# Identity matmuls and a reordered Wo fold in the prologue, x2 transfers issued ahead of stores, and three down jobs among the last output projections of a decoder-layer kernel

## The reference

```python
q, k, v = heads(x @ Wq.T), heads(x @ Wk.T), heads(x @ Wv.T)      # 16 heads of 32
q_r, k_r, v_r = q @ Wdown, k @ Wdown, v @ Wdown                  # rank 32
attn = softmax(q_r @ k_r.T / sqrt(32))
out = heads_back((attn @ v_r) @ Wup) @ Wo.T
x = layernorm(x + out)
r[s] = decay * r[s-1] + ctx[s] * ctx[s]                          # per head, along the sequence
x = layernorm(x + x * r)
inter = silu(x @ gate_w.T) * (x @ up_w.T)                        # 512 -> 2048
x = layernorm(x + inter @ down_w.T)                              # 2048 -> 512
```

## Time and profile before

| | us |
|---|---|
| runs | 713.72, 713.31, 709.81 |
| median | 713.31 |
| profiled execution | 709.71 |
| its span, first to last instruction | 707.2 |
| PE busy | 657.8 (93%) |
| DVE busy | 442.3 |
| ACT busy | 348.5 |
| POOL busy | 289.2 |

### The profile page before, as it was taken

The page is one execution under the profiler, slowest core; times in us unless marked ns, Lnnn a source line. Parts: engine busy times, 40 slices in busy tenths (PEclk is TensorE's granted clock), DMA queues, the critical chain, the costliest instruction groups (busy, mean ns, idle before and its releaser), DMA issues.

```text
span 707.2 us, 11967 instructions
## 1 busy us (share of the span) xinstructions
PE 657.8 (93%) x4284; PEld 537.4 (76%) x4284; DVE 442.3 (63%) x827; ACT 348.5 (49%) x1001; POOL 289.2 (41%) x350
## 2 busy tenths in 40 slices
PE   6899999999999999999687789999999999999994
PEld 6678787887878887887555567888888888888883
DVE  2257667697676877868767676765554555454434
ACT  4555656556466675675655554653333334332220
POOL 0744475987639568485743642500010001000103
PEclk9999999999999999999989898999999999999998
DMA  9530101200212120121302362555163515440301
GB/s 330 182 125 31 61 1 31 90 32 1 90 61 91 40 69 12 61 70 41 99 1 68 96 156 70 115 146 126 31 172 88 127 30 164 99 97 0 120 0 59
DMA packets 22010, 58.04 MB, mean 82 GB/s; under 512 B 4033, under 2 KB 7233, under 8 KB 21057
## 3 DMA queue, kind: packets, MB, share of 16 engines
q1 hardware_dynamic: 16720, 44.45, 21.9%
q0 software_dynamic: 4944, 12.32, 5.9%
q10 hardware_dynamic: 288, 0.52, 0.3%
HBM read 32.11 MB, written 8.39 MB: 57 GB/s over the span
## 4 chain that ended last, share of the span: by engine, by line
PE 85%; DVE 6%; ACT 3%; DMA 2%; issue 1%; POOL 1%; SPq 1%; ACTq 0%; DVEq 0%; POOLq 0%
PE bank L302 21%; PE bank L303 19%; PE bank L304 19%; PE bank L486 7%; PE bank L508 5%; PE bank L474 5%; DVE minus_max L830 3%; PE bank L1201 2%; PE bank L1104 2%; DMA x_in<-x 1%; PE bank L494 1%; ACT probs L671 1%; PE bank L1173 1%; PE bank L399 1%; PE bank L525 1%
## 5 line engine op out<-in xcount | busy, mean ns | idle before, releaser
L671 ACT ACTIVATE probs<-bank,minus_max 128x256 f32<-128x256 f32 x256 | 117.2, 487 | 18.8 <-DVE minus_max L830 18.8
L302 PE MATMUL bank<-down,hidden_hi_lo 128*128 128x512 f32 x256 | 102.1, 399 | 0.0
L303 PE MATMUL bank<-down,hidden_hi_lo 128*128 128x512 f32 x256 | 101.0, 394 | 0.0
L304 PE MATMUL bank<-down,hidden_hi_lo 128*128 128x512 f32 x256 | 100.5, 392 | 0.0
L830 DVE TENSOR_REDUCE minus_max<-bank 128x2 f32<-128x512 f32 x128 | 79.4, 682 | 20.3 <-PE bank L474 20.3
L1402 DVE TENSOR_TENSOR hidden<-bank,silu 128x512 f32<-128x512 f32 x64 | 44.1, 690 | 63.5 <-PE bank L304 60.7
L1365 ACT ACTIVATE silu<-bank 128x512 f32<-128x512 f32 x64 | 38.3, 598 | 84.6 <-PE bank L304 83.7
L1406 DVE TENSOR_TENSOR hidden_hi_lo<-hidden,hidden_hi_lo 128x512 fp32r<-128x512 f32 x64 | 45.0, 703 | 41.2 <-ACT hidden_hi_lo L1378 41.1
L844 DVE COPY probsT<-bank 128x512 f32<-128x512 f32 x96 | 60.4, 682 | 10.9 <-PE bank L486 10.8
L1475 POOL TENSOR_TENSOR ffn_var_eps<-ffn_mean_var,constants 128x4 f32<-128x4 f32 x3 | 0.6, 198 | 158.9 <-DVE ffn_mean_var L1422 158.9
L486 PE MATMUL bank<-ident,probs 128*128 128x128 f32 x512 | 63.5, 278 | 2.0 <-ACT probs L671 2.0
(11 more groups left out here) (167 smaller groups left out, 1617.6 us busy)
## 6 DMA issues: line engine op xcount, KB each, us to landing
features_by_group<-features_by_cell SPq DMA_DIRECT2D x128, 128.0 KB, 2.4
ctx_squared_T<-in_ctxT SPq DMA_DIRECT2D x8, 512.0 KB, 3.3
xres<-in_x SPq DMA_DIRECT2D x8, 512.0 KB, 5.3
x_in<-x SPq DMA_DIRECT2D x16, 256.0 KB, 3.0
x_residual<-x POOLq DMA_DIRECT2D x4, 1024.0 KB, 9.1
out_x<-x_residual POOLq DMA_DIRECT2D x16, 256.0 KB, 2.8
xin_T<-in_xT SPq DMA_DIRECT2D x7, 512.0 KB, 4.2
x<-x_rows SPq DMA_DIRECT2D x7, 512.0 KB, 3.0
```

Of the source, the lines that this page charges most:

```text
L302: nc.tensor.matmul(out, wh, xh, start=first, stop=False)
L303: nc.tensor.matmul(out, wh, xl, start=False, stop=False)
L304: return nc.tensor.matmul(out, wl, xh, start=False, stop=last)
L671: inc(nc.scalar.activation(probs[:, g, t, :], S[g][:, t * T:(t + 1) * T], ACT.Exp, bias=nmax[:, g, t:t + 1], accum_out=rsum[:, t, g:g + 1] ...
```

## The change

Four parts.

1. **Prologue.** PE multiplies the identity by itself 14 times (`pe_warm`, into bank 4, read by nobody) as soon as the identity is there. The diagonals' two products move from PE's start to behind the first half of the K projection. Of the Wo fold one product stays ahead of the first transposes, two go behind them, one goes behind `pe_r`; ACT's copies of V and casts of Wo and DVE's low parts of Wo go behind the exponentials and the copies of the heads.
2. **x2 transfers.** In batch 7 SP issues `xres` and the x2 rows t = 2 and 3 first, and the store of batch 5 after them. For blocks 1 to 3 the rows t = 0 and 1 go between the two halves of the feature transfers of the block before. The transposes of rows t = 2 of block 0 move from head group 1 to head group 2 of batch 7.
3. **Hand-over to the FFN.** The function table with silu is loaded in batch 7, behind the exponentials of the last head group, by a one-column activation. The last product of the moments goes behind the running sum's transposes. Job 18 joins 16 and 17: one before, one between, one behind the two output projections.
4. **First step.** With three jobs made ahead, step 0 has two jobs instead of four, the second of them behind the gate and up products of j = 1. Each later step still has four until they run out, one job further on.

```diff
-    FOLD_O, XB = (A_, B_, C_, A_), (B_, A_, C_, C_)
+    FOLD_O, XB = (C_, B_, A_, C_), (B_, A_, C_, C_)
+    WARM = 14
+    def pe_warm(pe):
+        pe.wait_ge(s_ident, 1)
+        for i in range(WARM):
+            nc.tensor.matmul(bank[4][:, 0:P], ident[:], ident[:], start=True, stop=True)
...
 def pe_first_k(pe):
...
+            if k == 1:
+                pe_diagonals(pe)
...
 def pe_fold_o(pe, m):
         if m == 0:
             pe.wait_ge(s_wo, 16)
-            pe.wait_ge(s["vc"], 1)
-        elif m == 1:
+            pe.wait_ge(s["qwl"], 3)
+        elif m == 3:
+            pe.wait_ge(s["owl"], 1)
+        else:
             pe.wait_ge(s["vc"], 2)
-        elif m == 2:
-            pe.wait_ge(s["qwl"], 3)
-        else:
-            pe.wait_ge(s["owl"], 1)
...
 def act_batch(act, b):
...
         act_extra_hi(act, b, 2)
+        if not proj:
+            nc.scalar.activation(silu_ready[:], nmax[:, 0, 0:1], ACT.Silu)
         act_heads(act, b, 3)
...
 def sp_batch(sp, b):
...
+        if b == B - 1:
+            wait(sp, "r1", 2 * b)
+            inc(sp.dma_start(xres[:], x_v[:, b, :, :]), "xres", 16)
+            for t in range(2, BT):
+                sp_x2in(sp, 0, t)
+            sp_store(sp, b - 2)
+            return
...
-    AHEAD_JOBS = 2 * NG + 2
+    AHEAD_JOBS = 2 * NG + 3
...
 def pe_down(pe, step, t):
-                pe.wait_ge(s["wld"], 2 * JT * (g + 1) - 2)
+                pe.wait_ge(s["wld"], 2 * JT * g + 1)
...
 def job_of(n, g, k):
-        i = AHEAD_JOBS + 2 * JT * g + k
-        return i if n == 0 and i < NJOB else None
+        i = AHEAD_JOBS + (2 * JT * g - 2 + k if g else k)
+        return i if n == 0 and i < NJOB and (g or k < 2) else None
...
 def pe_step(pe, n, g):
         pe_down(pe, prev, 1)
-        pe_fill(pe, n, g, 1)
+        if prev:
+            pe_fill(pe, n, g, 1)
         pe_turn(pe, n, g, 1)
         pe_gate_up(pe, n, g, 1)
-        pe_fill(pe, n, g, 2)
+        pe_fill(pe, n, g, 2 if prev else 1)
...
             pe_rs(pe, B - 1, 0)
             pe_rs(pe, B - 1, 1)
-            pe_o(pe, B - 1, 0)
+            pe_features(pe, 0, 3, A_)
             pe.wait_ge(s["yv"], 4 * B)
             pe_job(pe, 2 * NG, X)
-            pe_o(pe, B - 1, 1)
+            pe_o(pe, B - 1, 0)
             pe.wait_ge(s["ws"], 2 * NG + 1)
             pe_job(pe, 2 * NG + 1, X)
+            pe_o(pe, B - 1, 1)
+            pe.wait_ge(s["ws"], 2 * NG + 2)
+            pe_job(pe, 2 * NG + 2, X)
```

More of the change, by code:

```diff
@@ L425, in pe_q @@
             pe.wait_ge(s["xl"], 2 * nb + 2)
-            pe.wait_ge(s["owl"], 3)
+            pe.wait_ge(s["owl"], 4)
             wait(pe, "rs1", 2 * nb - 3)
@@ L554, in pe_batch @@
         if b == 0:
-            for m in range(MT):
-                pe_fold_o(pe, m)
+            pe_fold_o(pe, 0)
         else:
@@ L561, in pe_batch @@
         pe_t(pe, b, 0)
+        if b == 0:
+            pe_fold_o(pe, 1)
+            pe_fold_o(pe, 2)
         if post:
@@ L567, in pe_batch @@
         pe_extra(pe, b, 0)
+        if b == 0:
+            pe_fold_o(pe, 3)
         pe_pv(pe, b, 0)
@@ L595, in pe_batch @@
         else:
+            pe_xt(pe, 0, 2, B_)
             pe_xt(pe, 0, 3, A_)
@@ L707, in act_batch @@
         if b == 0:
+            act_v(act, 0, 0)
+            act_v(act, 0, 1)
+        act_heads(act, b, 0)
+        if b == 0:
             for m in range(MT):
                 act_weight_hi(act, "o", m)
-        act_heads(act, b, 0)
         if post:
@@ L848, in dve_batch @@
         dve_max(dve, b, 0)
-        if b == 0:
-            for m in range(MT):
-                dve_weight_lo(dve, "o", m)
         dve_extra(dve, b - 1, 3)
@@ L859, in dve_batch @@
         dve_heads(dve, b, 0)
+        if b == 0:
+            for m in range(MT):
+                dve_weight_lo(dve, "o", m)
         dve_y(dve, b, 0)
@@ L873, in dve_batch @@
         dve_max(dve, b, 2)
-        if not proj:
-            dve_x2l(dve, 0, 2, B_)
         dve_extra(dve, b, 1)
@@ L1385, in act_step @@
         act_fill_hi(act, n, g, 0)
-        act_fill(act, n, g, 1)
-        act_turn(act, n, g, 1)
-        act_fill_hi(act, n, g, 1)
-        act_silu(act, n, g, 1)
+        if before(n, g):
+            act_fill(act, n, g, 1)
+            act_turn(act, n, g, 1)
+            act_fill_hi(act, n, g, 1)
+            act_silu(act, n, g, 1)
+        else:
+            act_silu(act, n, g, 1)
+            act_fill(act, n, g, 1)
+            act_fill_hi(act, n, g, 1)
         act_fill(act, n, g, 2)
@@ L1442, in dve_step @@
         dve_fill_lo(dve, n, g, 0)
-        dve_fill(dve, n, g, 1)
-        dve_turn(dve, n, g, 1)
-        dve_fill_lo(dve, n, g, 1)
-        dve_hm(dve, n, g, 1)
+        if before(n, g):
+            dve_fill(dve, n, g, 1)
+            dve_turn(dve, n, g, 1)
+            dve_fill_lo(dve, n, g, 1)
+            dve_hm(dve, n, g, 1)
+        else:
+            dve_hm(dve, n, g, 1)
+            dve_fill(dve, n, g, 1)
+            dve_fill_lo(dve, n, g, 1)
         dve_fill(dve, n, g, 2)
@@ L1653, in _ @@
                 sp_batch(sp, b)
-            for t in range(2, BT):
-                sp_x2in(sp, 0, t)
             for g in range(QUAD):
@@ L1659, in _ @@
             sp_store(sp, B - 2)
+            for t in range(2):
+                sp_x2in(sp, 1, t)
             for c in range(CELLS):
@@ L1663, in _ @@
             for n in range(1, NB):
-                for t in range(BT):
+                for t in range(2, BT):
                     sp_x2in(sp, n, t)
@@ L1670, in _ @@
                     sp_store(sp, B - 1)
+                if n + 1 < NB:
+                    for t in range(2):
+                        sp_x2in(sp, n + 1, t)
                 for c in range(CELLS):
```

15 lines of the change are left out of this document (7 added, 8 removed).

## The result

The changed kernel takes **689.37 us** (median of 4 runs, 689.23 to 690.51) against 712.56 us (709.81 to 713.72) for the kernel before, run on the same chip beside it: ratio 0.968, 95% interval 0.965 to 0.972. The forecast was 690.0 us. A second set on another occasion gave 689.34 against 710.61 us, 0.970 (0.968 to 0.972).

The account below looks back on a forecast made before the run. PE, busy for 93% of 707.2 us, was taken as the bound. Gains 5.1 + 5.2 + 4.5 + 6.7 = 21.5 us from the profiled 709.7 gave 688.2, plus 1.8 made 690.0; own spread 685.5 to 693, to 697 for 8 in 10.

Parts of the forecast that it names:

- Prologue: Start through batch 0's first attention times V, which would end at 37.0 instead of 42.1 us: gain 5.1 us.
- The order: Prologue: exponentials ahead of V copies and Wo casts, most Wo folds later; 4.0 of the prologue's 5.1 us.
- the warm-up: Kernel start: identity products let K's 48 matmuls pass at the fast pitch; net gain 1.1 us with the diagonals moved.
- The rival drawn from it: Kernel start: with only 6 slow matmuls the warm-up is worth 0.2 us and the sum 20.6; no chance given.
- x2 rows, block 0: Batch 7, head group 1: rows issued earlier end PE's 6.4 us wait; gain 5.2 us, clock included.
- block 1: FFN, x2 rows issued near 399 instead of 422.36 us: idle 4.7 and half of 4.0 go; gain 6.7 us.
- Hand-over and first step: Attention to FFN: first down product 8.7 us behind the first gate product; gain 4.5 us.
- The table load: Batch 7's last group: the 1.28 us silu load fits ACT's 1.45 us idle but for 0.1; with drain, sum 20.3.
- The 1.8 us between the profiled execution and the median: Whole kernel: half of the 3.6 us by which the median stood above the profiled execution, added to 688.2.
- The clock rival: Thinned stretches (31 to 36, 347 to 354, 389 to 398 us): two clock falls, about 2 us each, 692 to 695; chance 0.15.
- Holes only change their names: Prologue and hand-over lose as much as they win, only x2 parts pay (11.9): 697.8, median 699.6; chance 0.12.
- 60 us at 0.50: Slower rival: PE stays at 1.2 GHz from the hand-over into the dense FFN, giving 721 us; chance 0.03.

Follow-up runs that it names:

- e_prologue: The kernel before with the prologue alone changed (14 identity products, diagonals moved, Wo fold, V copies and Wo casts reordered): 706.12 us, ratio 0.993.
- e_nowarm: The changed kernel without the 14 identity products at its start: 691.34 us.
- e_hand: The kernel before with the hand-over alone changed (silu table, last moments product, job 18 ahead, two jobs in step 0): 706.36 us, ratio 0.994.
- e_fill: The kernel before with 18 identity products ahead of PE's wait for the x2 rows of block 1: 709.75 us, ratio 0.998.
- e_notable: The changed kernel without the one-column activation in batch 7, so the silu table loads at its first use: 690.91 us.
- e_x2: The kernel before with the x2 transfers alone moved, and the transposes of t = 2 one head group later: 698.77 us, ratio 0.984.
- r_after: The changed kernel run again without any edit, as the base for other runs: 689.34 us.
- r_cast0: Second run of the changed kernel with ACT's cast of the first Wo product ahead of its copies of the heads: 688.46 us, ratio 0.967.
- e_cast0: First run of the changed kernel with ACT's cast of the first Wo product moved ahead of its copies of the heads: 688.53 us.
- e_hold: The kernel of e_cast0 with identity products in PE's short holes of batch 7, head groups 1 and 2: 687.59 us, ratio 0.966.

## Why the prediction was right, and where it was off

- **Prologue: 5.1 forecast, 3.8 in the trace (4.6 by the medians of e_prologue).** The order was right and so was the new wait: "PE stands behind ACT and DVE for some 1.8 us there", measured 1.7. What was off is a size, "PE's last fold product (0.56)". The row read for it, 1.13 us x2 in the earlier trace rows, holds two records of *one* float32 product, not two products. So the last fold takes 1.1 us (36.14 to 37.20), 0.5 more than forecast. The two folds ahead of the inverse's transposes take 2.0 us instead of 1.1; ACT waits 1.8 us for those transposes, so that its copies, the cast, the low part and with them the last fold come 0.8 us later (36.1 against 35.3). Attention times V ended at 38.3 against the 37.0 forecast, which is the 1.3 us missing. By the medians of e_prologue nothing is missing, but their interval (3.3 to 6.8 us) holds both figures.
- **The two halves of it.** Net of the moved diagonals the warm-up gave 14.47 - 13.36 = 1.1 us, the figure of the forecast. From the fold of Wq to the second scores pass 24.84 us instead of 27.54: the order gave 2.7 against 4.0, and the 1.3 between is the folds' size. How much the warm-up gives depends on the run it is set against: by the four profiled executions with the old prologue (10 to 19 matmuls at half rate) 0.5 to 1.5 us, by e_nowarm 2.3. The Trainium skill (TensorE: Matmul & The Clock Gate, What's actually happening) warns that this number differs from run to run and must not be fitted to; the four traces agree. The rival drawn from it (6 of them, a warm-up worth 0.2) is near what e_hand's execution would have given. What holds in the traces with the 14 products is K at the fast pitch from its first matmul, which takes that scatter away.
- **x2 rows, block 0: 5.2 forecast, 5.1 measured; block 1: 6.7 and 6.4.** Both walks hold: the chain without the stall is the length of a group that never had it plus 1.1 us (10.55 against 9.47), where 0.9 were forecast. That these are the norm statistics on DVE, as the forecast had it, no run tests. At block 1 nothing else was late. The half rate behind the stall, half of 4.0, is shown on its own by e_fill (2.07).
- **Hand-over and first step: 4.5 forecast, 4.4 measured.** The first down product stands 8.75 us behind the first gate product, forecast 8.7. What the walk had at one place is spread over several: PE waits 1.7 us in all for three jobs, the longest 0.8, and 1.5 us for the low part of the second hidden values. The forecast took the wait of step 1 to be even with what the low clock had cost there; it was 0.5 us worse, so that 3.9 of the 4.4 are left at step 2.
- **The table load.** It hides as forecast. e_notable prices it at 0.8 us in the trace and 1.6 by the medians. The Trainium skill (ScalarE: Activation LUTs, What ACT_TABLE_LOAD costs) adds a drain of about 1.38 us to a switch. No row shows it: silu starts 0.01 us behind a load of 1.28 in e_notable, and in the changed kernel the one-column activation follows 0.02 us behind. The prediction's reason, "as ACT had nothing in flight", is not quite what the rows show: in both places, and in the kernel before, a cast of 0.4 us had ended 0.02 us ahead of the load. Behind a short cast, then, the load has no drain beside it; what one behind longer work costs, no run here shows.
- **The 1.8 us between the profiled execution and the median** was a guess, and wrong: the changed kernel's median stands 0.1 above its profiled run. It happened to make up for the prologue: 688.2 was forecast for the profiled run and 689.3 measured, 1.1 too good, and the 1.8 on top were 1.7 too many. That the median came within 0.6 us of 690.0 is luck in this part; the gain of the profiled run, 21.5 forecast and 20.4 measured, is the fairer test. That the distance would shrink with the stalls was right: before spans 3.6 to 4.5 us within a set, the changed kernel 1.3 to 1.5. Whether it is the clock behind the stalls that spreads the runs stays open: over the runs of before the span and the mean granted clock correlate at -0.46 (17 runs beside e_x2), -0.03 (9 beside r_after) and -0.59 (9 beside r_cast0).
- **The clock rival (0.15)** did not decide the changed kernel, but it is real: it took about 1 us of e_cast0. Why the clock fell there and not in the two traces of the changed kernel, with the same work in the same stretch 1.9 us earlier, stays open. It need not be a property of the kernel: it falls in some executions of either (the slowest run of r_after has a mean clock of 0.989). In the one trace of e_hold filler kept it up, and e_fill shows the same in a long stall; that filler does so in every run is not shown.
- **"Holes only change their names"** fell, since the prologue and the hand-over pay 4.6 and 4.4 us on their own. A trace of it exists: 1 us of e_hand went into the stall behind.
- **Two sums of the rivals** are slightly off: 60 us at 0.50 lose 30, which from 690.0 gives 720 and not 721, and a load that sticks out by 1.3 leaves 20.2 and not 20.3. Nothing hangs on either.

## What to carry to other kernels

Walk from stall to stall in order of time. Idle time plus half of the busy time at the low clock behind it is the most that a stall can give back; what it does give is set by the chain that is late next. At block 1, where PE itself was next, the bound was 6.7 us and 6.4 came; at block 0 it was 8.8 (6.4 + half of 4.8) and 5.1 came, at the hand-over 8.5 and 4.4, since there ACT and DVE were next. After a fix, look for the next stall that would swallow it, as block 1's did in e_hand. Issue a transfer when its buffer comes free, not where its turn in a long list of others stands. Where a stretch has to wait often and briefly, identity products in the holes can keep the clock; here they cost nothing, even at twice their planned length, because other engines set the pace. Read a row's "x2" as records: a float32 product leaves two.

## What the runs showed of the hardware

- A float32 product leaves two records: 18 of 128x128 leave 36 records in 4.18 us (e_fill), two of 128x512 leave four in 1.98 us.
- The granted clock column reads 1.00 in the first 12 us while matmuls pass at half the rate (one in 0.21 us against 0.12). With 14 float32 identity products, from 1.5 to 6.8 us, the pitch is 0.12 from K's first products on.
- With one and the same prologue 10, 17, 17 and 19 matmuls passed at half rate in four executions before the pitch rose; behind the identity products none did.
- Two kernels with the same work and the same busy time in a stretch (6.97 and 6.99 us of ten) had 0.85 to 0.87 and 1.00 of the clock there, in two traces each; with the holes filled (9.54 us, one trace) it was 1.00. A fall to 0.83 in group 3 (e_cast0, e_notable) cost nothing.
- With 4.2 us of identity products in a stall the granted clock behind it was 1.00 instead of 0.50, and the work up to the next rows took 3.28 us instead of 5.35.
- A function table load takes ACT 1.28 us, 0.02 us behind a short cast, and the activation starts 0.01 to 0.02 us behind it.
